# The skip term of y moved from a TensorE matmul to ScalarE, the convolution carries gathered on GpSimd, and a whole third B product on GpSimd in nine groups

## The chip, the cores and the metric

The kernel runs on one core of a Trainium2 chip. The core has TensorE (PE, matrix products into PSUM), VectorE (DVE), ScalarE (ACT), GpSimd (POOL) and SyncE (SP, which issues DMAs); each works through its own instruction stream in order and waits for the others on semaphores. The metric is the device time of one execution, in microseconds; lower is better.

## The reference

Two blocks follow each other on x of shape (2, 1024, 512). The first is a Mamba block; only its middle matters here:

```python
xs, res = jnp.split(xn @ W_in, 2, axis=-1)            # 1024 channels each
xs = silu(causal_conv(xs, conv_w) + conv_b)            # 4 taps, depthwise
delta = softplus(dt_r @ W_dt + b_dt)
h = h * exp(delta * A) + delta * B * u                 # scan over time, 16 states a channel; u = xs
y = einsum(h, C) + u * D                               # the skip term is u * D
y = y * silu(res);  out = y @ W_out + x
```

The second block is a mixture of 32 experts (top 4 of 32, 2048 tokens, and a shared expert). The change does not touch it.

## The kernel before, in words

Time is cut into NSEG = 4 segments of 512 steps (two for each sequence), and the 1024 channels into DC = 8 tiles of 128 partitions. One pair of segment s and tile d is a group, g = 8s + d, from 0 to 31. The scans go through the groups one after the other, each with its 16 states in four quarters q of 4 states. For one group the engines do this:

- ScalarE: `decay(g, q)` writes four factors exp(delta * A) into four PSUM banks `da`, each as soon as VectorE has done with the bank's last content; `silu_z` and `silu_x` need another activation table, so a table load stands ahead of and behind them; `tap` makes the first of the four convolution taps of a tile of the next segment; `softplus` makes the next group's delta; `spread_du` copies `du` into PSUM.
- VectorE: `spread(g, q)` makes du * B for a quarter (128x2048), `scans(g, q)` runs four scans (L945), `gate(g-1)` multiplies the last group's y by silu(res), and `conv` makes the other three taps (L914, each waits for the one before it).
- GpSimd: `weigh(g, q)` multiplies a quarter by C (L1342, and folds it in two in some groups, L1347), `delta_x` makes delta and du for the next group, and `spread` makes the quarters that `by_pool` gives to it.
- TensorE: `summed(g, q)` adds the quarter's four states into the bank `y_ps` with an identity matrix (L1542), and between the quarters it runs the work of `gap_items`: input projections for the next segment ("in", L1439), its gate projection ("z", L1471), delta ("dt", L1476), output projections of the last segment ("out", L1461), transposes. A float32 product of 128x512 stands in the trace as two matmul records, so a block of four is a row of x8.

Who makes a product with B depends on the group. `dense` groups (d = 3, 4, 5 of segments 0 to 2: groups 3, 4, 5, 11, 12, 13, 19, 20, 21) carry most of the "in" items and so the convolutions. `leaving` groups (d = 0 to 2 of segments 1 to 3) carry the "out" items. Ahead of its quarter 0 each group has the skip term: TensorE waits for `gate(g-1)`, which frees `y_ps`, and multiplies the diagonal matrix `d_diag` by xs (L1539).

A segment with s even is the first half of a sequence; there VectorE also makes the carry into the next segment, three small instructions for each tile that stand between the taps (L908). In odd segments it adds this carry to the first three columns (L911).

The order of each engine's work is written out in the program's loops over g and q; no planner moves it. The functions that the change touches, and what calls them:

## Time and profile before

| | |
|---|---|
| median of 3 runs | 1617.28 us (1613.62 to 1618.94) |
| profiled execution, its own time | 1620.9 us |
| its span in the profile | 1618.9 us |
| busy in the span | PE 1449.8, DVE 1308.3, ACT 741.5, POOL 1077.6 us |
| the scans of groups 0 to 31 | from 72 to 996 us of the span |

Busy time is a mean over stages with different limits. The scans take the first 996 us; the rest is the routing and the experts. Times in rows are microseconds from the start of the span; a row such as "4.57 ... [0.16 <-ACT bank L717]" says that the instructions took 4.57 us and that the engine had stood idle for 0.16 us before, until ScalarE's line 717 released it.

### The profile page before, as it was taken

Reading aid. Unit: us, or ns where it says so; the run is one execution under the profiler, and the core shown is the slowest. Engines: PE = TensorE matmul, PEld = TensorE weight load, DVE = VectorE, ACT = ScalarE, POOL = GpSimd, SP = SyncE. Lnnn points to the kernel's source line nnn. Section 1 sums busy time; section 2 is a strip of 40 time slices with the busy share of each in tenths; the row PEclk is TensorE's granted clock in tenths of the full one; section 3 lists DMA queues with packets and bytes.
Section 4 is the critical chain, followed back from the end, with each engine's and each line's share of the span. In section 5 each row is a group of like instructions: output and inputs, shape, how many; then the busy total and the mean of one; then the engine's idle time right before and its main releaser. Section 6 shows DMA issues by size and latency. Waiting matters only on the chain. (4 is left out here: it accounts for less than half of the span.)

```text
span 1618.9 us, 14732 instructions
## 1 busy us (share of the span) xinstructions
PE 1449.8 (90%) x4412; PEld 725.0 (45%) x4413; DVE 1308.3 (81%) x1931; ACT 741.5 (46%) x1160; POOL 1077.6 (67%) x545
## 2 busy tenths in 40 slices
PE   6578998889998889998798878899998999999996
PEld 3233443334443334443343323444445766667774
DVE  4599999999999999999999997355636777777772
ACT  4566665776656776657566664421000111111111
POOL 0199898999887999989999997230011455555453
PEclk9889999899999999999899999999999999999998
DMA  4540112410113411103310004021412888888895
GB/s 131 221 174 9 42 48 101 179 40 30 35 47 108 171 41 36 35 15 126 129 36 21 28 1 156 20 104 33 182 54 64 225 237 225 218 239 223 259 260 68
DMA packets 63823, 176.86 MB, mean 109 GB/s; under 512 B 10304, under 2 KB 15168, under 8 KB 55040
## 3 DMA queue, kind: packets, MB, share of 16 engines
q1 hardware_dynamic: 48128, 138.59, 24.8%
q0 software_dynamic: 15616, 37.32, 11.1%
q8 instruction: 37, 0.61, 0.2%
q14 instruction: 42, 0.34, 0.1%
HBM read 142.98 MB, written 32.85 MB: 109 GB/s over the span
## 5 line engine op out<-in xcount | busy, mean ns | idle before, releaser
L1342 POOL TENSOR_TENSOR h<-h,c_rep 128x2048 f32<-128x2048 f32 x128 | 579.3, 4530 | 31.2 <-DVE h L945 26.1
L1542 PE MATMUL bank<-h,ident 128*128 128x512 f32 x916 | 449.3, 634 | 93.0 <-POOL h L1342 74.2
L717 ACT ACTIVATE bank<-delta,a_neg 128x512 f32<-128x512 f32 x512 | 335.8, 682 | 178.9 <-DVE h L945 178.1
L1542 PEld LDWEIGHTS bank<-h,ident 128*128 128x128 f32 x916 | 180.6, 202 | 335.9 <-issue 210.9
L945 DVE TENSOR_TENSOR_SCAN h<-bank,state,h 128x512 f32<-128x512 f32 x256 | 306.0, 1260 | 0.5 <-ACT bank L717 0.5
L945 DVE TENSOR_TENSOR_SCAN h<-bank,h 128x512 f32<-128x512 f32 x256 | 290.7, 1199 | 2.8 <-ACT bank L717 2.6
L171 DVE STREAM_TRANSPOSE xT<-xg 32x256 f32<-32x256 f32 (+1 forms) x592 | 247.3, 418 | 56.0 <-DMA xg<-flat,slot_token 48.3
L935 DVE TENSOR_TENSOR h<-bank,b_rep 128x2048 f32<-128x2048 f32 (+1 forms) x105 | 227.5, 2184 | 35.7 <-ACT bank L708 24.2
L1703 POOL DMA_INDIRECT out<-y,slot_token x64 | 101.8, 1590 | 110.1 <-DMA out<-y,slot_token 65.2
L1329 POOL TENSOR_TENSOR h<-du,b_rep 128x2048 f32<-128x2048 f32 (+1 forms) x32 | 125.4, 3920 | 11.5 <-PE bank L1542 11.5
L1787 ACT ACTIVATE y<-y_ps,share 128x512 f32<-128x512 f32 x69 | 47.4, 687 | 185.3 <-PE y_ps L1935 152.3
L1439 PE MATMUL bank<-xnT,w_in 128*128 128x512 f32 x256 | 120.4, 616 | 10.1 <-ACT zs L680 9.2
L1893 PE MATMUL g_ps<-xT,w_ring 128*128 128x256 f32 x512 | 119.4, 387 | 8.2 <-issue 4.3
L1471 PE MATMUL bank<-xnT,w_res 128*128 128x512 f32 x256 | 118.6, 607 | 0.1
L1461 PE MATMUL bank<-w_out,xs 128*128 128x512 f32 x256 | 115.6, 594 | 1.5 <-DVE xs L955 0.9
L1893 PEld LDWEIGHTS g_ps<-xT,w_ring 128*128 128x128 f32 x512 | 98.9, 194 | 38.1 <-issue 25.6
L1893 PE MATMUL u_ps<-xT,w_ring 128*128 128x256 f32 x512 | 115.7, 379 | 0.0
L1935 PE MATMUL y_ps<-w_ring,act 128*128 128x512 f32 x256 | 115.4, 594 | 0.0
L1893 PEld LDWEIGHTS u_ps<-xT,w_ring 128*128 128x128 f32 x512 | 96.9, 190 | 13.0
L1695 POOL DMA_INDIRECT xg<-flat,slot_token x65 | 64.9, 998 | 50.9 <-POOLq L411 25.6
L1407 POOL DMA_INDIRECT xg<-flat,slot_token x4 | 4.0, 1012 | 135.4 <-DVE slot_token L1210 134.5
L1439 PEld LDWEIGHTS bank<-xnT,w_in 128*128 128x128 f32 x256 | 49.9, 197 | 76.6 <-issue 62.4
(238 smaller groups left out, 1530.0 us busy)
## 6 DMA issues: line engine op xcount, KB each, us to landing
w_ring<-in_w SPq DMA_DIRECT2D x32, 1024.0 KB, 5.3
b_rep<-bcd SPq DMA_DIRECT2D x16, 1024.0 KB, 6.9
c_rep<-bcd SPq DMA_DIRECT2D x16, 1024.0 KB, 5.0
w_ring<-in_w SPq DMA_DIRECT2D x32, 512.0 KB, 7.4
w_in<-in_w_in_x SPq DMA_DIRECT2D x32, 256.0 KB, 2.6
w_res<-in_w_in_res SPq DMA_DIRECT2D x32, 256.0 KB, 2.6
xa<-in_x SPq DMA_DIRECT2D x20, 256.0 KB, 3.0
xb<-in_x SPq DMA_DIRECT2D x16, 256.0 KB, 3.0
```

Source lines behind the costliest of these rows:

```text
L171: ins = eng.transpose(out[cols:cols + PIECE, 0:slots, :, rows:rows + PIECE], x[rows:rows + PIECE, :, :, cols:cols + PIECE])
L717: eng.activation(da[j][:], delta[:, g % 2], ACT.Exp, scale=a_neg[:, col:col + 1])\
L935: eng.tensor_tensor(h[:, q, a:b], du_ps[:].unsqueeze(1).to_broadcast([P, b - a, SEG]), b_rep[:, Q * q + a:Q * q + b, :], ALU.mult).then_in ...
L945: eng.tensor_tensor_scan(h[:, q, j, :], da[j][:], h[:, q, j, :], init, ALU.mult, ALU.add)\
L1329: eng.tensor_tensor(h[:, q, a:b], du[:].unsqueeze(1).to_broadcast([P, b - a, SEG]), b_rep[:, Q * q + a:Q * q + b, :], ALU.mult).then_inc(S ...
L1342: ins = eng.tensor_tensor(h[:, q], h[:, q], c_rep[:, Q * q:Q * q + Q, :], ALU.mult)
L1439: ins = eng.matmul(out[:], w_in[:, n % 2, k, :], xnT[:, s % 2, k, :], start=(k == 0), stop=(k == KC - 1))
L1461: eng.matmul(out[:], xs[:, s % 2, d, i * P:(i + 1) * P], w_out[:, d, :], start=(d == 0), stop=False)
L1471: ins = eng.matmul(out[:], w_res[:, i % 2, k, :], xnT[:, s % 2, k, :], start=(k == 0), stop=(k == KC - 1))
L1542: ins = eng.matmul(y_ps[:], c.ident[:], h[:, q, j, :], start=False, stop=(q == NQ - 1 and j == Q - 1))
L1893: ins = eng.matmul(out[:, f * 2 * P:(f + 1) * 2 * P], c.w1r[:, own, k, first + f * P:first + (f + 1) * P], xT[:, u % 2, k, :], start=(k == ...
L1935: ins = eng.matmul(y_ps[i][:], turned[:, k, v * P:(v + 1) * P], c.w2r[:, places(n)[0] % RING, k, :], start=(k == 0), stop=(k == FC - 1))
```

## The change

The change has three parts.

1. The skip term. In place of the matmul with `d_diag`, ScalarE writes xs times D straight into `y_ps` (`skip_term`), once `gate(g-1)` is done, and TensorE's sums then add to what stands there. ScalarE does it in each group but the first, behind `decay(g, 2)` and ahead of the taps and of `softplus`. Only one of the eight diagonal blocks is still made.
2. The carries. In even segments ScalarE copies the last three columns of each convolution input to `conv_edge` right behind the tap, and GpSimd makes the carries of all eight tiles at once in six small instructions (`tails`), in groups 1 and 17. VectorE's three small instructions for each tile go.
3. The third quarter's B product in the nine dense groups: GpSimd makes all four states, where before it made two and VectorE the other two.

```diff
@@ -128,6 +128,7 @@
         b_dt, d_skip = new("b_dt_sb", [P, DC]), new("d_skip", [P, DC])
         a_neg, norm_w = new("a_neg", [P, DC * NS]), new("norm_w_a", [P, KC])
         tail, bc, state = new("conv_tail", [P, DC, KW - 1]), new("bc", [P, P]), new("state", [P, DC * NS])
+        edge, part = new("conv_edge", [P, DC, KW - 1]), new("conv_part", [P, KW - 1, DC, KW - 1])
         st6, mv = new("st6", [P, NSEG, ST, 6]), new("mv", [P, NSEG, ST, 2])
         eps_ln, eps_rms, minus = new("eps_ln", [P, 1]), new("eps_rms", [P, 1]), new("minus", [P, ST])
         lnv, rvar, ms = new("lnv", [P, ST]), new("rvar", [P, ST]), new("ms", [P, ST])
@@ -228,11 +229,11 @@
         gu_ps = [(bank[0], bank[1]), (bank[2], bank[3])]
         PLACED, RESTED, LISTED = E, 2 * E, 2 * E + 2 * REST
 
-        names = ("const_ready small_loaded aneg_ready diag_ready xp_loaded out_loaded stat_done mv_ready ln_chain "
+        names = ("const_ready small_loaded aneg_ready diag_ready xp_loaded out_loaded stat_done carry_made mv_ready ln_chain "
                  "rvar_ready ms_ready rrms_ready scales_ready pool_chain xn_ready tap_done "
                  "conv_chain xs_ready bcd_written sp_chain sp_ready delta_ready "
                  "du_made du_ready bq_made b3_made da_ready scan_done state_saved weighed cmul_done y_summed gate_done "
-                 "xr_ready").split()
+                 "xr_ready skip_made").split()
         S = {n: sem("m_" + n) for n in names}
         b_loaded = [sem(f"m_b_loaded{q}") for q in range(NQ)]
         c_loaded = [sem(f"m_c_loaded{q}") for q in range(NQ)]
@@ -274,7 +275,7 @@
                 return (0, 0)
             if q == NQ - 1:
                 return (0, Q)
-            return (Q // 2, Q) if q == NQ - 2 and dense(g) else (0, 0)
+            return (0, Q) if q == NQ - 2 and dense(g) else (0, 0)
 
         def by_vector(g, q):
             a, b = by_pool(g, q)
@@ -666,8 +667,11 @@
 
                 def tap(s, j):
                     ps, _ = filled(eng, "in", s, j)
-                    eng.activation(xs[:, s % 2, j, :], ps[:], ACT.Identity, scale=conv_w[:, j, KW - 1:KW],
-                                   bias=conv_b[:, j:j + 1]).then_inc(S["tap_done"], 1)
+                    ins = eng.activation(xs[:, s % 2, j, :], ps[:], ACT.Identity, scale=conv_w[:, j, KW - 1:KW], bias=conv_b[:, j:j + 1])
+                    if s % 2 == 0:
+                        after(eng, S["carry_made"], s // 2 * 2 * (KW - 1))
+                        ins = eng.activation(edge[:, j, :], ps[:, SEG - KW + 1:SEG], ACT.Copy)
+                    ins.then_inc(S["tap_done"], 1)
 
                 def silu_x(s, j):
                     read(eng, "in", s, j)
@@ -698,6 +702,11 @@
                     eng.activation(spl[:], spl[:], ACT.Exp, scale=-1.0).then_inc(S["sp_chain"], 1)
                     eng.wait_ge(S["sp_chain"], g * 2 + 2)
                     eng.activation(spl[:], spl[:], ACT.Ln, bias=c.ones[:, 0:1]).then_inc(S["sp_ready"], 1)
+
+                def skip_term(g):
+                    s, d = divmod(g, DC)
+                    eng.wait_ge(S["gate_done"], g)
+                    eng.activation(y_ps[:], xs[:, s % 2, d, :], ACT.Copy, scale=d_skip[:, d:d + 1]).then_inc(S["skip_made"], 1)
 
                 def spread_du(g):
                     eng.wait_ge(S["du_made"], g + 1)
@@ -728,8 +737,7 @@
                 layer_var(1)
                 root_mean(1)
                 eng.wait_ge(c.made, 4)
-                for d in range(DC):
-                    ins = eng.activation(d_diag[:, d, :], c.ident[:], ACT.Copy, scale=d_skip[:, d:d + 1])
+                ins = eng.activation(d_diag[:, 0, :], c.ident[:], ACT.Copy, scale=d_skip[:, 0:1])
                 ins.then_inc(S["diag_ready"], 1)
                 for j in range(DC):
                     tap(0, j)
@@ -772,6 +780,8 @@
                     if d == DC - 1 and s + 2 < NSEG:
                         root_mean(s + 2)
                     decay(g, 2)
+                    if g:
+                        skip_term(g)
                     for it in gap_of(g - 1, 3, "in"):
                         tap(it[1], it[2])
                     for it in gap_of(g - 1, 3, "out", 1):
@@ -902,12 +912,8 @@
                     p, x, w = work[u], xs[:, s % 2, j, :], conv_w
                     eng.wait_ge(S["tap_done"], n + 1)
                     for sft in range(1, KW):
-                        if s % 2 == 0:
-                            k = KW - sft
-                            old = conv_b[:, j:j + 1].to_broadcast([P, KW - 1]) if sft == 1 else tail[:, j, 0:k]
-                            link(eng.scalar_tensor_tensor(tail[:, j, 0:k], p[:, SEG - k:SEG], w[:, j, sft - 1:sft], old,
-                                                          ALU.mult, ALU.add))
-                        elif sft == 1:
+                        if s % 2 and sft == 1:
+                            eng.wait_ge(S["carry_made"], (s // 2 + 1) * 2 * (KW - 1))
                             link(eng.scalar_tensor_tensor(x[:, 0:KW - 1], p[:, 0:KW - 1], w[:, j, KW - 1:KW], tail[:, j, :],
                                                           ALU.mult, ALU.add))
                             eng.wait_ge(S["conv_chain"], links[0])
@@ -1347,6 +1353,23 @@
                         ins = eng.tensor_tensor(h[:, q, 0:Q // 2], h[:, q, 0:Q // 2], h[:, q, Q // 2:], ALU.add)
                     ins.then_inc(S["cmul_done"], 1)
 
+                def tails(s):
+
+                    eng.wait_ge(S["tap_done"], (s + 1) * DC)
+                    made = s // 2 * 2 * (KW - 1)
+                    for sft in range(1, KW):
+                        k = KW - sft
+                        eng.tensor_tensor(part[:, sft - 1, :, 0:k], edge[:, :, sft - 1:KW - 1],
+                                          conv_w[:, :, sft - 1:sft].to_broadcast([P, DC, k]), ALU.mult).then_inc(S["carry_made"], 1)
+                    eng.wait_ge(S["carry_made"], made + KW - 1)
+                    eng.tensor_tensor(tail[:], part[:, 0], conv_b[:].unsqueeze(2).to_broadcast([P, DC, KW - 1]), ALU.add)\
+                        .then_inc(S["carry_made"], 1)
+                    for sft in range(2, KW):
+                        k = KW - sft
+                        eng.wait_ge(S["carry_made"], made + KW - 1 + sft - 1)
+                        eng.tensor_tensor(tail[:, :, 0:k], tail[:, :, 0:k], part[:, sft - 1, :, 0:k], ALU.add)\
+                            .then_inc(S["carry_made"], 1)
+
                 weighed = [0]
                 for s in (0, 1):
                     mean_square(s)
@@ -1356,6 +1379,8 @@
                     s, d = divmod(g, DC)
                     if d == DC - 1:
                         mean_square(s + 2)
+                    if d == 1 and s % 2 == 0:
+                        tails(s)
                     spread(g, 2)
                     weigh(g, 0)
                     spread(g, 3)
@@ -1532,14 +1557,16 @@
                     s, d = divmod(g, DC)
                     if g == 0 and q == 0:
                         was_free(eng, 5)
-                    if q == 0:
-                        after(eng, S["gate_done"], g)
+                    if q == 0 and g == 0:
                         eng.wait_ge(S["diag_ready"], 1)
                         eng.wait_ge(S["xs_ready"], g + 1)
                         eng.matmul(y_ps[:], d_diag[:, d, :], xs[:, s % 2, d, :], start=True, stop=False)
+                    elif q == 0:
+                        eng.wait_ge(S["skip_made"], g)
                     eng.wait_ge(S["cmul_done"], g * NQ + q + 1)
                     for j in range(Q // 2 if folded(g, q) else Q):
-                        ins = eng.matmul(y_ps[:], c.ident[:], h[:, q, j, :], start=False, stop=(q == NQ - 1 and j == Q - 1))
+                        ins = eng.matmul(y_ps[:], c.ident[:], h[:, q, j, :], start=False, stop=(q == NQ - 1 and j == Q - 1),
+                                         skip_group_check=g > 0)
                     ins.then_inc(S["y_summed"], 1)
 
                 for it in opening:
```

On ScalarE, in group 4, before (from `silu_z` to the last quarter's decays; `bank` is a PSUM bank, `zs` silu(res), `spl` and `delta` the parts of softplus):

```order
L680 ACTIVATE zs<-bank 128x512
L675 ACTIVATE xs<-xs 128x512 x3
L771 ACT_TABLE_LOAD
L717 ACTIVATE bank<-delta,a_neg 128x512 x4
L669 ACTIVATE xs<-bank,conv_b_sb,conv_w_sb 128x512
L695 ACTIVATE spl<-bank,b_dt_sb 128x512
```

and in the changed kernel, at the same place:

```order
L684 ACTIVATE zs<-bank 128x512
L679 ACTIVATE xs<-xs 128x512 x3
L779 ACT_TABLE_LOAD
L726 ACTIVATE bank<-delta,a_neg 128x512 x4
L709 ACTIVATE bank<-xs,d_skip 128x512
L670 ACTIVATE xs<-bank,conv_b_sb,conv_w_sb 128x512
L699 ACTIVATE spl<-bank,b_dt_sb 128x512
```

The skip term (L709) stands behind the four decays of quarter 2 and ahead of the tap.

On TensorE, in group 4, before (from the "dt" item of the group before to quarter 1's sums; `ident` is the identity matrix):

```order
L1476 MATMUL bank<-dtr,w_dt_sb 128x512
L1439 MATMUL bank<-xnT,w_in 128x512 x4
L1539 MATMUL bank<-xs,d_diag 128x512
L1542 MATMUL bank<-h,ident 128x512 x4
L1439 MATMUL bank<-xnT,w_in 128x512 x4
L1542 MATMUL bank<-h,ident 128x512 x4
```

and in the changed kernel:

```order
L1501 MATMUL bank<-dtr,w_dt_sb 128x512
L1464 MATMUL bank<-xnT,w_in 128x512 x4
L1568 MATMUL bank<-h,ident 128x512 x4
L1464 MATMUL bank<-xnT,w_in 128x512 x4
L1568 MATMUL bank<-h,ident 128x512 x4
```

The skip matmul is gone, and nothing else moved; the first sums now wait for ScalarE's L709.

On GpSimd, from quarter 3 of group 2 to quarter 0 of group 3 and on to quarter 3's product with B, before (`du` times `b_rep` is the product with B, `h` times `c_rep` the weighing with C):

```order
L1342 TENSOR_TENSOR h<-h,c_rep 128x2048
L1329 TENSOR_TENSOR h<-du,b_rep 128x1024
L1339 TENSOR_TENSOR state<-h,ones 128x4
L1342 TENSOR_TENSOR h<-h,c_rep 128x2048
L1329 TENSOR_TENSOR h<-du,b_rep 128x2048
```

and in the changed kernel:

```order
L1348 TENSOR_TENSOR h<-h,c_rep 128x2048
L1335 TENSOR_TENSOR h<-du,b_rep 128x2048
L1345 TENSOR_TENSOR state<-h,ones 128x4
L1348 TENSOR_TENSOR h<-h,c_rep 128x2048
L1335 TENSOR_TENSOR h<-du,b_rep 128x2048
```

The product with B ahead of quarter 0's weighing has twice the columns.

## Rows read from the trace of the kernel before

**Rows 1.** The page's strip of VectorE's busy tenths, 40 slices of the span

```profile
DVE  4599999999999999999999997355636777777772
```

**Rows 2.** Busy time by window, a window for each group: 3, 4, 11, 12, 13, 18, 19, 20

```profile
core 0: us, PE busy (x) PEld busy (x) DVE busy (x) ACT busy (x) POOL busy (x), PEclk, DMA share, GB/s
...
153.54:188.28 34.74, 34.74 (x82) 15.37 (x82) 31.52 (x33) 18.65 (x27) 34.26 (x14) 1.00 0.11 33
188.28:219.92 31.64, 29.72 (x69) 12.47 (x68) 31.16 (x33) 20.12 (x30) 27.08 (x13) 1.00 0.12 36
...
391.31:424.69 33.38, 33.38 (x78) 14.88 (x79) 32.61 (x39) 19.98 (x31) 33.21 (x10) 1.00 0.14 42
424.69:457.83 33.14, 31.15 (x69) 13.43 (x68) 32.62 (x40) 20.09 (x30) 27.84 (x9) 0.95 0.12 34
457.83:487.96 30.13, 28.14 (x62) 12.08 (x61) 29.99 (x33) 19.31 (x29) 25.26 (x8) 0.94 0.15 46
...
600.40:630.02 29.62, 28.15 (x64) 12.40 (x64) 27.43 (x22) 18.75 (x30) 28.90 (x14) 0.94 0.06 20
630.02:664.49 34.47, 33.23 (x76) 14.38 (x77) 31.46 (x34) 20.04 (x32) 33.91 (x16) 1.00 0.15 40
664.49:696.13 31.64, 30.29 (x70) 12.78 (x69) 31.17 (x33) 20.11 (x30) 28.33 (x13) 1.00 0.12 36
```

**Rows 3.** Timeline of VectorE in group 4: start, us, engine, line

```profile
192.76 1.20 DVE L935 TENSOR_TENSOR h<-bank,b_rep 128x1024 f32<-128x1024 f32 x1
...
199.16 4.57 DVE L945 TENSOR_TENSOR_SCAN h<-bank,h 128x512 f32<-128x512 f32 x4 [0.16 <-ACT bank L717]
...
215.49 2.32 DVE L914 SCALAR_TENSOR_TENSOR xs<-bank,conv_w_sb,xs 128x511 f32<-128x511 f32 x3
```

**Rows 4.** Timeline of ScalarE in group 4

```profile
198.34 2.52 ACT L717 ACTIVATE bank<-delta,a_neg 128x512 f32<-128x512 f32 x4
...
214.20 0.78 ACT L669 ACTIVATE xs<-bank,conv_b_sb,conv_w_sb 128x512 f32<-128x512 f32 x1 [1.49 <-PE bank L1439]
```

**Rows 5.** Timeline of TensorE in group 4

```profile
195.53 3.70 PE L1439 MATMUL bank<-xnT,w_in 128*128 128x512 f32 x8 [1.62 <-ACT zs L680]
199.06 1.12 PE L1539 MATMUL bank<-xs,d_diag 128*128 128x512 f32 x2
...
210.57 3.60 PE L1439 MATMUL bank<-xnT,w_in 128*128 128x512 f32 x8
```

**Rows 6.** ScalarE's groups by line and shape: busy us, mean ns, idle before

```profile
L708 ACT ACTIVATE bank<-du 128x512 f32<-128x512 f32 x32 | 19.2, 600 | 75.4 <-POOL du L1318 75.4
...
L1787 ACT ACTIVATE y<-y_ps,share 128x512 f32<-128x512 f32 x67 | 46.0, 687 | 183.2 <-PE y_ps L1935 150.2 <-PE y_ps L1879 23.4 <-DMA out<-y,slot_token 8.1
```

**Rows 7.** Timeline of TensorE at 432 and at 751 us, a block behind an idle stretch

```profile
432.18 5.40 PE L1439 MATMUL bank<-xnT,w_in 128*128 128x512 f32 x8 [1.99 <-ACT zs L680]
...
751.48 3.70 PE L1542 MATMUL bank<-h,ident 128*128 128x512 f32 x8 [2.73 <-POOL h L1342]
```

**Rows 8.** Timeline of VectorE in group 11, one convolution with its carries

```profile
407.15 0.19 DVE L908 SCALAR_TENSOR_TENSOR conv_tail<-bank,conv_w_sb,conv_b_sb 128x3 f32<-128x3 f32 x1
...
409.74 4.80 DVE L945 TENSOR_TENSOR_SCAN h<-bank,state,h 128x512 f32<-128x512 f32 x4
```

**Rows 9.** GpSimd's products with B by shape, scans of all groups

```profile
L1329 POOL TENSOR_TENSOR h<-du,b_rep 128x2048 f32<-128x2048 f32 x23 | 104.1, 4528 | 10.5 <-PE bank L1542 10.5
...
L1329 POOL TENSOR_TENSOR h<-du,b_rep 128x1024 f32<-128x1024 f32 x9 | 21.3, 2366 | 1.0 <-PE bank L1542 1.0
```

**Rows 10.** Timeline of GpSimd in group 3, then early in group 17

```profile
175.71 1.27 POOL L1318 TENSOR_TENSOR du<-delta,xs 128x512 f32<-128x512 f32 x1 [0.17 <-POOL delta L1314]
...
577.34 0.21 POOL L1339 TENSOR_TENSOR state<-h,ones 128x4 f32<-128x4 f32 x1
577.63 4.52 POOL L1342 TENSOR_TENSOR h<-h,c_rep 128x2048 f32<-128x2048 f32 x1
```

**Rows 11.** Timeline of VectorE: opening, and end of group 3

```profile
51.74 0.22 DVE L908 SCALAR_TENSOR_TENSOR conv_tail<-bank,conv_w_sb,conv_b_sb 128x3 f32<-128x3 f32 x1 [2.15 <-ACT xs L669]
...
179.22 2.28 DVE L935 TENSOR_TENSOR h<-bank,b_rep 128x2048 f32<-128x2048 f32 x1
```

## The prediction

> **What bounds the kernel now.** I read the strip of busy tenths first: VectorE is at nine tenths or more through nearly all of the scans [rows 1]. That says who is busy, not who sets the pace, so I cut the scans into one window for each group [rows 2]. The reader is to see three kinds there. In groups 3 and 11 TensorE is busy the whole window (34.74 of 34.74 us, 33.38 of 33.38) and GpSimd nearly so (34.26, 33.21), while VectorE is not. In groups 4, 12, 13 and 20 VectorE has all but 0.1 to 0.5 us, GpSimd has 3.3 to 5.3 us to spare and TensorE only 1.4 to 2.0. In group 18 GpSimd is the fullest (28.90 of 29.62). So each part of the change meets a group in which its receiver has no room, and what VectorE is relieved of counts only where nobody else comes last. For that I read the timeline of group 4.
>
> **The half product with B that VectorE loses.** It is one instruction of 1.20 us at 192.76, in each of nine groups [rows 3]. The next scans but four start at 199.16 and already wait 0.16 us for ScalarE's decays [rows 3], whose batch starts at 198.34 [rows 4]. That batch stands behind two table loads and three silus that start once quarter 0's scans are through, ahead of the half product. Without the half product VectorE only waits longer, 1.3 instead of 0.16 us. The gain in groups 4, 5, 20 and 21 is nothing; in groups 12 and 13, whose scans are longer, I take 0.15 us each. The bound below is that all 9 x 1.1 = 9.9 us are lost as gain, the bound above that they are kept.
>
> **The skip term.** TensorE saves the two records at 199.06, about 1.0 us, in 31 groups. But it started its sums behind them at 200.05, and now waits for ScalarE, where the skip term stands behind the whole batch of decays: 198.34 + 2.52 = 200.86 [rows 4, 5]. No activation from SBUF to PSUM with a scale of its own stands in the trace for Copy; between 0.60 us (a plain copy from SBUF into PSUM) and 0.69 us (a copy with a scale out of PSUM) [rows 6] I take 0.65. So the sums start at about 201.6, 1.5 us later. (The Trainium skill, "ScalarE: Activation LUTs", section "Rules for kernel authors", budgets about 0.3 us for each activation and 0.83 ns an element, which makes an estimate of 0.72 us for 512; by it each such group would be 0.07 us longer still. The rows here are shorter, so I keep them.)
>
> Who waits for these sums? Four blocks of TensorE follow without a gap (sums, "in", sums, "in"), the last at 210.57 for 3.60 us; ScalarE's tap waited 1.49 us for it at 214.20, and VectorE's convolution at 215.49 came right behind [rows 3 to 5]. The tap ends at 214.98 and the taps of the convolution start 0.5 us later with a small instruction (0.2 us) between, so only 0.3 us is slack, and closer packing of the blocks gives 0.2 more. Groups 4 and 20 become 1.5 - 0.5 = 1.0 us longer each. In group 12 the same chain is met by carries that leave VectorE: a convolution with its carries takes 409.74 - 407.15 = 2.59 us, three taps alone 2.32 less the overlap, 2.23, so 0.36 us for each convolution [rows 3, 8]; the copy of the edge adds about 0.2 us to the tap. I take -0.2 us for group 12, and for group 13, whose two convolutions have slack behind TensorE, -0.15 - 0.7 = -0.8. In groups without convolutions the gate comes behind the decays, and skip copy (0.65) and skip matmul (1.0) change places with nothing behind them late: 0.
>
> **The clock.** The wait opens an idle stretch on TensorE that was not there. Its "in" block starts when ScalarE frees the bank (195.53 [rows 5]) and ends near 199.1; then it idles until 201.6, 2.5 us. What such a stretch does the trace shows both ways: behind 1.99 us of idleness eight records took 5.40 us, in a group whose mean granted clock is 0.95, not 1.00 [rows 2, 7], so part of them ran at 1.2 in place of 2.4 GHz; behind 2.73 us they took 3.70 [rows 7]. At 5.40 the chain above is 1.75 us longer. I take the fall for the three groups 4, 12 and 20, 5.25 us, and 0.5 us in each of 5, 13 and 21, where the block is followed by a convolution that has over a microsecond of slack, 1.5 us. The bounds are 0 and 6.75.
>
> **The whole product on GpSimd.** Twice the states cost 4.53 - 2.37 = 2.16 us in each of nine groups [rows 9]. Groups 4, 12, 13 and 20 leave GpSimd 3.3 to 5.3 us idle [rows 2], most of it right behind this product, where it waits for quarter 0's scans, and groups 5 and 21 are built alike: 0. In the first group of each run GpSimd comes from a full stretch and hands the 2.16 us on through weigh 0, spread 3 and weigh 1 to du. In group 3 du ended at 176.98, its copy would end at 177.6 and VectorE took it at 179.22 [rows 10, 11]: 1.6 us slack, 0.6 late; TensorE's second sums, which wait for weigh 1, then delay "in" and the third convolution a little more: +0.8. In group 11 TensorE has no idle time at all [rows 2], so its second sums come 1.8 us late and "in", tap and third convolution with them; the carries give back 0.3: +1.5. Group 19 follows groups that GpSimd already fills: +2.0. Sum 4.3, bounds 0 and 3 x 2.16 = 6.5, and 3.4 more if TensorE's clock falls in groups 11 and 19, where it would idle some 2.1 us ahead of its second sums.
>
> **The carries on GpSimd.** Six instructions of 0.20 us, of which some wait for the one before: such a pair has a pitch of 0.29 us (577.34 to 577.63 [rows 10]); between 6 x 0.20 and 6 x 0.29 I take 1.4. In group 17 they stand exactly in this gap, on the fullest engine, and what VectorE and TensorE do through group 18 follows it: +1.4. In group 1 GpSimd waits for TensorE behind them: +0.2. In the opening VectorE waited 2.15 us ahead of each convolution [rows 11], so the carries that it no longer makes count only in the last tile: -0.2.
>
> **Sum.** Without the clock 2.0 - 0.2 - 0.8 + 4.3 + 1.4 + 0.2 - 0.2 = 6.7 us, with it 6.7 + 6.75 = 13.4 us. Against the profiled execution's own 1620.9 that is 1634.3. This execution lies 3.6 us above the median of the runs shown, 1617.28, so a median of 1631 is what I forecast.
>
> **The rivals.**
> (a) The clock does not fall in the new gaps: +6.7, 1624. For it speaks the row at 751 us, against it the one at 432 [rows 7]. It shares its chance, 0.24, over +2 to +10 us.
> (b) The other side: VectorE is the bound and keeps what it is relieved of. Then 9 x 1.1 for the half products and 24 x 0.12 for the carries in the scans come off, 12.8 us: 1604.5. What decides is the start of TensorE's first sums in group 4: if they start no later than 11.8 us behind the group's first scan, as now, and the third batch of scans before 10.9 us, this is right. For it speaks the strip [rows 1] and VectorE's 31.16 of 31.64; against it the 0.16 us [rows 3]. Chance 0.12.
> (c) Each engine's slack eats both sides, within 4.8 us: 1617. The saved 1.0 us of TensorE in the groups with "out" items, where it is nearly full too (28.15 of 29.62 in group 18 [rows 2]), would pay for the delays. Chance 0.12.
> (d) The clock falls in groups 11 and 19 too, and GpSimd's delay passes in full: 13.4 + 3.4 + 2.2 = +19, 1636. Chance 0.10.
> The forecast itself, +10 to +17: 0.42.
>
> **How the numbers follow.** A measurement of this kernel tells 0.3%, 4.9 us, from no change. Faster: (b), 0.12. Same: (c) and a third of (a), 0.20. Slower: 0.68. The range for 8 in 10 leaves out most of (b) and the far end of (d): 1613 to 1637. The forecast's own is 1627 to 1634.
>
> **What would show it.** Right: the first sums of group 4 start about 13.3 us behind its first scan, VectorE waits over 1 us for ScalarE ahead of the third batch of scans in groups 4, 5, 20 and 21, and again for the tap ahead of the third convolution; groups 4 and 20 last 34 us, or 32.7 if the clock holds; group 19 about 36.5; group 17 and 18 together 1.4 us more. Wrong: groups 4 and 20 at 30.5 us, or a skip activation that starts before the decays' batch has ended.

## The result: 0.9% slower, as forecast

The changed kernel takes 1631.36 us (median of 6 runs, 1627.62 to 1632.17), the kernel before 1616.53 us in 6 runs beside it (1613.62 to 1618.94). The ratio is 1.0088, 95% interval 1.0067 to 1.011. The forecast was 1631 with 1613 to 1637. (Two single runs lie far outside all others, 1928.11 us of the kernel before and 5172.87 us of the kernel with the three mends below; the ratios leave them out, the medians hold them.)

The profiled execution took 1631.55 us, its span is 1629.9. I read the windows first, one for each group, the same groups as [rows 2], with 28 behind them:

```profile
core 0: us, PE busy (x) PEld busy (x) DVE busy (x) ACT busy (x) POOL busy (x), PEclk, DMA share, GB/s
155.44:191.11 35.67, 33.84 (x79) 14.49 (x79) 30.39 (x33) 19.27 (x28) 35.19 (x14) 1.00 0.11 32
191.11:225.60 34.49, 31.14 (x69) 13.30 (x68) 30.24 (x33) 20.63 (x31) 31.66 (x13) 0.95 0.11 33
396.11:431.23 35.12, 34.20 (x75) 14.69 (x76) 30.54 (x30) 19.47 (x31) 34.95 (x11) 0.95 0.13 38
431.23:465.62 34.39, 30.71 (x68) 13.10 (x67) 30.55 (x30) 20.80 (x34) 30.33 (x9) 0.95 0.11 33
465.62:494.97 29.35, 25.36 (x59) 10.86 (x58) 28.19 (x27) 19.96 (x32) 27.07 (x8) 1.00 0.16 48
607.95:639.20 31.25, 28.04 (x62) 12.38 (x62) 27.55 (x23) 19.35 (x32) 30.05 (x14) 0.89 0.06 19
639.20:675.63 36.43, 32.63 (x74) 13.92 (x75) 30.38 (x33) 19.91 (x30) 35.87 (x16) 1.00 0.13 38
675.63:710.11 34.48, 31.12 (x69) 13.28 (x68) 30.23 (x33) 20.63 (x31) 31.67 (x13) 0.95 0.11 33
905.24:933.85 28.61, 21.96 (x43) 8.92 (x42) 26.21 (x21) 16.96 (x25) 24.98 (x8) 0.88 0.04 12
```

In group 4 VectorE was busy for all but 0.48 us; now it is idle for 4.25 of 34.49 us. It does 0.9 us less and the group lasts 2.85 us longer. In groups 3 and 19 GpSimd fills the window (35.19 of 35.67, 35.87 of 36.43), and TensorE, which was full in group 3, is not any more: the bound has changed engines.

The timelines of group 4 answer to [rows 3 to 5]. VectorE:

```profile
191.06 9.01 DVE L951 TENSOR_TENSOR_SCAN h<-bank,h 128x512 f32<-128x512 f32 x8
199.99 0.66 DVE L961 TENSOR_TENSOR xs<-bank,zs 128x512 f32<-128x512 f32 x1
201.92 4.57 DVE L951 TENSOR_TENSOR_SCAN h<-bank,h 128x512 f32<-128x512 f32 x4 [1.26 <-ACT bank L726]
...
220.87 0.22 DVE L917 SCALAR_TENSOR_TENSOR xs<-bank,conv_w_sb,conv_tail 128x3 f32<-128x3 f32 x1 [2.10 <-ACT xs L670]
```

ScalarE:

```profile
201.13 2.53 ACT L726 ACTIVATE bank<-delta,a_neg 128x512 f32<-128x512 f32 x4
203.59 0.67 ACT L709 ACTIVATE bank<-xs,d_skip 128x512 f32<-128x512 f32 x1
...
220.05 0.78 ACT L670 ACTIVATE xs<-bank,conv_b_sb,conv_w_sb 128x512 f32<-128x512 f32 x1 [3.15 <-PE bank L1464]
```

TensorE:

```profile
198.31 3.70 PE L1464 MATMUL bank<-xnT,w_in 128*128 128x512 f32 x8 [1.04 <-ACT zs L684]
204.32 5.40 PE L1568 MATMUL bank<-h,ident 128*128 128x512 f32 x8 [2.31 <-ACT bank L709]
...
216.42 3.60 PE L1464 MATMUL bank<-xnT,w_in 128*128 128x512 f32 x8
```

Read them across. The gate (L961) has freed `y_ps` at 200.65. The skip term starts at 203.59, because it stands behind four decays, which stand behind the table load. TensorE waits for it, 2.31 us, and then runs its eight records in 5.40 us. The "in" block at 216.42 comes 25.36 us behind the first scan (before: 210.57 against 188.28, 22.29), the tap waits 3.15 us for it, and the convolution waits 2.10 us for the tap. The 1.20 us product that VectorE no longer makes comes back as the 1.26 us that it waits for the third batch of decays.

The other end of the change, GpSimd in group 17 and VectorE in group 19:

```profile
584.34 0.59 POOL L1362 TENSOR_TENSOR conv_part<-conv_edge,conv_w_sb 128x24 f32<-128x24 f32 x3
585.01 0.23 POOL L1365 TENSOR_TENSOR conv_tail<-conv_part,conv_b_sb 128x24 f32<-128x24 f32 x1
585.31 0.52 POOL L1370 TENSOR_TENSOR conv_tail<-conv_tail,conv_part 128x16 f32<-128x16 f32 x2
585.78 0.20 POOL L1345 TENSOR_TENSOR state<-h,ones 128x4 f32<-128x4 f32 x1
```

```profile
658.18 4.57 DVE L951 TENSOR_TENSOR_SCAN h<-bank,h 128x512 f32<-128x512 f32 x4 [1.91 <-POOL h L1335]
...
666.23 2.29 DVE L941 TENSOR_TENSOR h<-bank,b_rep 128x2048 f32<-128x2048 f32 x1 [1.02 <-ACT bank L717]
```

The carries take 585.78 - 584.34 = 1.44 us with nothing else beside them. In group 19 VectorE waits 1.91 us for GpSimd's product, in a place where it waited for nobody before (there its scans followed a convolution without a wait, at 647.81).

The sum over the groups, from the group lengths of both traces: 3, 4, 5 +4.4 us; 11, 12, 13 +2.2; 17 and 18 +1.6; 19 +2.0; 20, 21 +3.5. That makes +13.7. All other groups together -2.1, the stretch ahead of the scans +1.7, behind them -2.4: the span is 11.0 us longer.

### The profile page after: what moved, and what is told of

It reads as the page before. It is cut to its first block and busy times, and to the rows that moved or that the text cites. A ratio compares the mean times of both kernels' runs of the same rounds, so it can differ in the third digit from the quotient of the medians.

```text
span 1629.9 us, 14619 instructions
## 1 busy us (share of the span) xinstructions
PE 1433.8 (88%) x4350; PEld 717.0 (44%) x4351; DVE 1293.4 (79%) x1874; ACT 758.5 (47%) x1200; POOL 1099.5 (67%) x557
## 5 line engine op out<-in xcount | busy, mean ns | idle before, releaser
L1568 PE MATMUL bank<-h,ident 128*128 128x512 f32 x916 | 462.7, 650 | 144.6 <-POOL h L1348 81.6
L941 DVE TENSOR_TENSOR h<-bank,b_rep 128x2048 f32<-128x2048 f32 x96 | 216.6, 2278 | 35.6 <-ACT bank L717 14.0
L1335 POOL TENSOR_TENSOR h<-du,b_rep 128x2048 f32<-128x2048 f32 x32 | 144.8, 4525 | 13.1 <-PE bank L1568 12.9
L920 DVE SCALAR_TENSOR_TENSOR xs<-bank,conv_w_sb,xs 128x511 f32<-128x511 f32 (+2 forms) x96 | 71.8, 747 | 25.6 <-ACT conv_edge L673 22.8
```

The costliest lines, as they stand in the source:

```text
L941: eng.tensor_tensor(h[:, q, a:b], du_ps[:].unsqueeze(1).to_broadcast([P, b - a, SEG]), b_rep[:, Q * q + a:Q * q + b, :], ALU.mult).then_in ...
L1335: eng.tensor_tensor(h[:, q, a:b], du[:].unsqueeze(1).to_broadcast([P, b - a, SEG]), b_rep[:, Q * q + a:Q * q + b, :], ALU.mult).then_inc(S ...
L1568: ins = eng.matmul(y_ps[:], c.ident[:], h[:, q, j, :], start=False, stop=(q == NQ - 1 and j == Q - 1), skip_group_check=g > 0)
```

## The experiments

Each was compared with runs of the kernel before on the same chip; ratios are to those: 28 runs, median 1619.51, for the three parts and the early skip term; 19 runs, 1617.27, for the filler, the half product in three groups, the earlier carries and the three mends; 29 runs, 1618.32, for the last three. The changed kernel itself had 1616.53 beside it, so medians of different sets are not subtracted from each other here. One kernel's runs lie up to 19 us apart and the intervals are 3 to 6 us wide on each side, so I judge each edit by the lengths of the groups it touches and use the ratio for the whole.

### One part at a time

**The skip term alone**, on the kernel before:

```diff
                     decay(g, 2)
+                    if g:
+                        skip_term(g)
...
-                    if q == 0:
-                        after(eng, S["gate_done"], g)
+                    if q == 0 and g == 0:
...
+                    elif q == 0:
+                        eng.wait_ge(S["skip_made"], g)
```

> The kernel before with the skip term alone moved to ScalarE. Theory (the skip term stands behind the decays, TensorE's sums come late and its clock falls in the new gap): about +8 us against before, with groups 4 and 20 at 34 to 34.5 us in place of 31.6 and group 12 near 34.5. Rival A (the loss of the change comes from GpSimd's added work alone): within 2 us of before. Rival B (TensorE is relieved and that pays): 5 us or more faster than before.

Measured: 1623.79 us, 1.0029 (0.9997 to 1.0061). Windows of groups 3, 4 and 20, then TensorE in group 4:

```profile
153.99:187.88 33.89, 33.89 (x79) 14.79 (x79) 31.43 (x34) 19.26 (x28) 33.41 (x14) 1.00 0.12 34
187.88:220.67 32.79, 29.05 (x68) 12.50 (x67) 31.27 (x34) 20.73 (x31) 29.08 (x13) 1.00 0.11 35
...
665.08:699.56 34.48, 30.86 (x68) 13.08 (x67) 31.37 (x34) 20.61 (x31) 29.24 (x13) 0.95 0.13 33
```

```profile
201.12 3.70 PE L1549 MATMUL bank<-h,ident 128*128 128x512 f32 x8 [2.30 <-ACT bank L705]
```

The wait is there, and costs 32.79 - 31.64 = 1.15 us without the clock. The fall behind it is not certain: the 2.30 us are followed by 3.70 us here, and group 20, of the same build, has a window at 0.95 that is 1.7 us longer. Group 3 shows what my sum lacked: TensorE is busy 33.89 of 33.89 us there, so the missing matmul shortens the group by 0.9 us.

**The whole B product alone:**

```diff
-            return (Q // 2, Q) if q == NQ - 2 and dense(g) else (0, 0)
+            return (0, Q) if q == NQ - 2 and dense(g) else (0, 0)
```

> The kernel before with the whole third B product on GpSimd in the nine dense groups, nothing else. Theory: groups 3, 11 and 19 get 1 to 2 us longer each, groups 4, 5, 20, 21 stay at 31.6 and 29.2 because ScalarE's decays come last, groups 12 and 13 gain 0.15 each: +3 to +4 us. Rival (VectorE keeps what it is relieved of): -8 to -10 us.

Measured: 1621.08 us, 1.0015 (0.9999 to 1.003). Groups 3 and 4:

```profile
153.56:189.20 35.64, 34.72 (x80) 14.90 (x80) 30.50 (x32) 18.64 (x27) 35.16 (x14) 1.00 0.12 32
189.20:220.82 31.62, 30.18 (x70) 12.86 (x69) 30.04 (x33) 20.12 (x30) 30.44 (x13) 1.00 0.13 36
```

Rival (b) falls here: with nothing else changed VectorE is relieved of 1.1 us in group 4 (30.04 against 31.16 busy) and the group lasts 31.62 us against 31.64. Groups 5, 20 and 21 are unchanged too. Group 12 gains 0.4, and that is a wait of VectorE for the tap, seen below, which the kernel before had and this build has not. Group 3 is 0.9 us longer, group 11 2.1, groups 17 to 19 together 1.6.

**The carries alone** (part 2 of the change):

```diff
+                    if s % 2 == 0:
+                        after(eng, S["carry_made"], s // 2 * 2 * (KW - 1))
+                        ins = eng.activation(edge[:, j, :], ps[:, SEG - KW + 1:SEG], ACT.Copy)
...
+                    if d == 1 and s % 2 == 0:
+                        tails(s)
```

> The kernel before with the carries alone moved to GpSimd. Theory: groups 12 and 13 lose 0.7 us each and group 11 0.3, group 17 with 18 gains 1.4 us: about 0 (-1 to +1) in all. Rival (what leaves VectorE is gained, and GpSimd's six small instructions are free): -3 us.

Measured: 1619.51 us, 1.0 (0.9981 to 1.002). Groups 12, 17 and 18:

```profile
424.56:456.16 31.60, 29.85 (x70) 12.81 (x69) 31.39 (x30) 20.30 (x33) 27.63 (x9) 1.00 0.12 36
...
568.43:599.61 31.18, 28.67 (x62) 12.57 (x62) 27.54 (x22) 19.56 (x31) 30.23 (x20) 0.89 0.16 53
599.61:627.54 27.93, 26.45 (x64) 11.82 (x64) 27.45 (x22) 19.13 (x31) 27.21 (x14) 1.00 0.07 21
```

Groups 17 to 19 are 2.6 us longer together, of which 1.44 are the six instructions; a clock of 0.89 in group 17 and 0.95 in 19 stand beside the rest. Group 12 is 1.5 us shorter. Here are one of its three convolutions and the start of the third on VectorE in the kernel before:

```profile
447.85 0.19 DVE L908 SCALAR_TENSOR_TENSOR conv_tail<-bank,conv_w_sb,conv_b_sb 128x3 f32<-128x3 f32 x1
...
450.43 2.28 DVE L935 TENSOR_TENSOR h<-bank,b_rep 128x2048 f32<-128x2048 f32 x1
453.02 0.22 DVE L908 SCALAR_TENSOR_TENSOR conv_tail<-bank,conv_w_sb,conv_b_sb 128x3 f32<-128x3 f32 x1 [0.31 <-ACT xs L669]
```

and the same convolution with the carries alone moved:

```profile
447.33 2.29 DVE L914 SCALAR_TENSOR_TENSOR xs<-bank,conv_w_sb,xs 128x511 f32<-128x511 f32 x3
449.55 2.28 DVE L935 TENSOR_TENSOR h<-bank,b_rep 128x2048 f32<-128x2048 f32 x1
```

The convolution takes 2.58 us from start to start in the one and 2.22 in the other, and VectorE, which waits for nobody in this group now, keeps that three times: 1.1 us. The other 0.4 us are the wait for the tap: the block of 5.40 us that the kernel before had at 432.18 [rows 7] took 3.70 here, and the tap no longer comes late. With the product alone no block of group 12 ran slow either, and it is 0.4 us shorter (32.72). Group 13, with two convolutions, is 0.75 us shorter.

The three parts alone add up to 0.4% in the ratios and the whole measures 0.9%. In the groups of the forecast they make 5.8, 4.0 and 0.3 us, 10.1 of 13.7. The missing 3.6 us are a balance. Group 4 is 1.7 us longer than its parts make it, because its block behind the new wait ran slow here and not with the skip term alone. Group 12 is 3.2 us longer: 1.6 are such a slow block, and the other 1.6 come because the late sums hold the group at 32.8 us (as the filler below shows), where the carries alone had brought it to 31.60. Group 3 adds 0.9, because GpSimd's delay covers what the missing matmul gave. Groups 11 and 17 to 19 take 2.3 back.

### Mending one part of the changed kernel

**The skip term earlier.** In groups 4 and 5 of each of the first three segments ScalarE writes it behind the first of the four decays, when the gate has just ended:

```diff
+                def early(g):
+                    return g // DC < NSEG - 1 and g % DC in (4, 5)
                 def decay(g, q):
                     for j in range(Q):
+                        if q == 2 and j == 1 and early(g):
+                            skip_term(g)
...
-                    if g:
+                    if g and not early(g):
                         skip_term(g)
```

> The changed kernel, but in groups 4, 5, 12, 13, 20 and 21 the skip term stands behind the first of the four decays of quarter 2 in place of behind the fourth. Theory: TensorE's first sums start about 11.5 us behind the group's first scan in place of 13.2, the idle stretch ahead of them shrinks from 2.3 to 0.6 us, the clock stays up, and groups 4, 12 and 20 come back to 31.5 to 32 us: 8 us faster than the changed kernel, still some 5 us slower than before. Rival (the place of the skip term does not matter, GpSimd sets the pace): within 2 us of the changed kernel.

Measured: 1623.85 us, 1.0027 (0.9997 to 1.0058). Groups 4 and 12, and TensorE in group 4:

```profile
189.42:221.07 31.65, 29.82 (x68) 12.32 (x67) 30.08 (x32) 20.73 (x31) 30.47 (x13) 1.00 0.12 36
...
427.01:458.58 31.57, 29.68 (x69) 12.60 (x68) 30.34 (x29) 20.91 (x34) 30.11 (x9) 1.00 0.12 36
```

```profile
200.83 3.70 PE L1573 MATMUL bank<-h,ident 128*128 128x512 f32 x8 [0.47 <-ACT bank L709]
```

The moved line gives back 2.8 us in each of groups 4, 12 and 20, 34.49 to 31.65 in group 4, and 0.65 in each of 5 and 21, with everything else left in: 9.8 us. That is the cause of the largest term, shown by taking it away. For the whole the ratio falls from 1.0088 to 1.0027, which is 9.9 us, with intervals of 3 to 5 us on each side. This profiled execution was one of the kernel's longest (1630.63 us of 1613.68 to 1632.45): it has groups 7, 16, 19 and 30 1.3 to 1.7 us longer than the changed kernel's, which the edit doesn't touch.

**The clock alone.** The wait stays, but TensorE is given less idleness: two redundant matmuls ahead of the "in" block, overwritten by the block itself:

```diff
+                        if s > 0 and i in (3, 6):
+                            for _ in range(2):
+                                eng.matmul(out[:], w_in[:, n % 2, 0, :], xnT[:, s % 2, 0, :], start=True, stop=True)
```

> The changed kernel with two more matmuls (four records, 1.7 us, their result overwritten) ahead of the input projection that TensorE does just before the idle stretch of groups 4, 5, 12, 13, 20 and 21. The sums can start no earlier by it; TensorE is only busy for longer before. Theory (the fallen clock is 1.75 us of each of groups 4, 12 and 20): the stretch shrinks from 2.3 to 0.6 us, the first sums take 3.6 and not 5.3 us, 5 us faster than the changed kernel. Rival (the late start alone costs, the clock is hidden): no faster, up to 2 us slower.

Measured: 1627.95 us, 1.0061 (1.0037 to 1.0085). Group 4, and TensorE in it:

```profile
188.78:221.57 32.79, 31.15 (x73) 13.45 (x72) 30.14 (x33) 20.73 (x31) 31.63 (x13) 1.00 0.11 35
```

```profile
196.02 1.98 PE L1465 MATMUL bank<-xnT,w_in 128*128 128x512 f32 x4 [1.05 <-ACT zs L684]
197.84 3.60 PE L1467 MATMUL bank<-xnT,w_in 128*128 128x512 f32 x8
202.03 3.70 PE L1571 MATMUL bank<-h,ident 128*128 128x512 f32 x8 [0.59 <-ACT bank L709]
```

The sums start 13.2 us behind the first scan, as in the changed kernel, but take 3.70 us. Group 4 is 1.70 us shorter and groups 12 and 20 are 1.6 and 1.7. So of the 2.85 us in group 4, 1.15 are the delay and 1.70 the clock. One group alone could not show that the filler did it, for group 4 lasts 32.79 us without a filler too, with the skip term alone and with the carries earlier. All six places do: behind 2.3 us of idleness 12 of 18 such blocks ran slow (5 of 6 in the changed kernel, 3 with the half product, 4 with the carries earlier), behind 0.59 us none of 6. The ratio of the whole does not stand apart from that of the changed kernel; the verdict rests on the groups.

**The half product again in groups 3, 11 and 19:**

```diff
-            return (0, Q) if q == NQ - 2 and dense(g) else (0, 0)
+            return (Q // 2 if g % DC == 3 else 0, Q) if q == NQ - 2 and dense(g) else (0, 0)
```

> The changed kernel, but in groups 3, 11 and 19 GpSimd makes only half of the third B product again. Theory: groups 3 and 11 lose 1 to 1.5 us each, group 19 2 us: 4 us faster than the changed kernel. Rival (the whole product costs in all nine groups alike, or nowhere): 1.4 us or less.

Measured: 1629.36 us, 1.0048 (1.001 to 1.0087). Groups 3 and 19:

```profile
153.12:187.00 33.88, 33.88 (x79) 14.78 (x79) 31.42 (x34) 19.25 (x28) 33.40 (x14) 1.00 0.12 34
634.23:668.47 34.24, 32.38 (x74) 14.00 (x75) 31.26 (x33) 19.91 (x30) 33.68 (x16) 1.00 0.15 41
```

Group 3 is 1.8 us shorter, group 19 2.2, group 11 1.0. (Groups 12 and 21 are shorter too, 1.6 and 0.7, where the edit does nothing: their blocks behind the wait took 3.70 here.) In group 3 it is not the 34.7 us of the kernel before that comes back but 33.88, TensorE full again and one matmul short. The two parts had hidden each other: the skip term's 0.9 us and GpSimd's 1.8.

**The carries of the second sequence three groups earlier**, in group 14 in place of 17. GpSimd is idle there for 4.4 of 28.77 us in the changed kernel:

```diff
-                    if d == 1 and s % 2 == 0:
-                        tails(s)
+                    if g == 1:
+                        tails(0)
+                    if g == 2 * DC - 2:
+                        tails(2)
```

> The changed kernel, but the six small carry instructions of segment 2 stand in group 14, where GpSimd has some 4 us idle, in place of group 17. Theory: 1.4 us of groups 17 to 19 go, group 14 keeps its length: 1.4 us faster than the changed kernel. Rival (they were hidden in group 17 too): no difference.

Measured: 1628.5 us, 1.006 (1.0042 to 1.0079). Group 14 lasts 28.78 us against 28.77, and groups 17 to 19 together are 2.1 us shorter (95.07 against 97.17), more than the 1.44 us moved; group 17 runs at a clock of 1.00 here against 0.94. TensorE in groups 4 and 20 of this one execution:

```profile
203.27 3.70 PE L1570 MATMUL bank<-h,ident 128*128 128x512 f32 x8 [2.31 <-ACT bank L709]
...
682.64 5.40 PE L1570 MATMUL bank<-h,ident 128*128 128x512 f32 x8 [2.30 <-ACT bank L709]
```

The same block behind the same wait, once at the high and once partly at the low clock. The edit does not touch either place.

### All mends together, and beyond

**The three mends in one kernel** (skip term early, half product in 3, 11 and 19, carries in 14), and the same kernel once more:

> The changed kernel with three mends: the skip term behind the first decay in the six groups with three or more silus, half the third product on GpSimd in groups 3, 11 and 19, the carries of segment 2 in group 14. Theory: 8 + 4 + 1.4 us faster than the changed kernel, that is 0 to 2 us faster than before, since half a microsecond to one of the removed matmul is kept in groups 3, 11 and 19. Rival (the mends overlap): 5 us slower than before or more.

> The kernel with the three mends once more, on the chip of the two beside it, for a narrower interval: 2 to 5 us faster than before; if its gain was chance, within 1 us of before.

Measured: 1614.79 us, 0.9967 (0.9941 to 0.9992), and 1616.23 us, 0.9985 (0.9967 to 1.0003). Group 7 and group 30 of the first execution, then of the second:

```profile
273.52:300.72 27.20, 19.66 (x44) 8.20 (x43) 25.13 (x21) 20.21 (x34) 25.34 (x18) 0.94 0.64 244
...
943.00:971.59 28.59, 21.94 (x43) 8.89 (x42) 26.21 (x21) 16.95 (x25) 24.96 (x8) 0.88 0.00 0
```

```profile
275.85:305.68 29.83, 23.84 (x48) 10.01 (x47) 25.22 (x21) 19.93 (x34) 26.60 (x18) 0.84 0.60 227
...
946.42:973.33 26.91, 18.84 (x43) 7.95 (x42) 26.10 (x22) 17.13 (x25) 24.98 (x8) 0.97 0.00 0
```

With the three costs taken away the 0.9% is gone: no interval reaches above 1.0003, with the rest of the change left in. In groups 17 to 19, though, the mends do not add up. Alone the half product takes 2.2 of 97.17 us off and the earlier carries 2.1, together only 1.9 and 2.7 in the two executions, with a clock of 0.91 in group 19; this stays open.

One and the same kernel, and group 7 differs by 2.6 us, group 30 by 1.7 the other way, each time with the lower clock at the longer one. The whole change is worth 15 us, and where the falls land moves 2 to 3 us in a single group that nobody edited.

**The half product in all nine groups**, with the other two mends: is there any gain in the six groups where GpSimd has room?

```diff
-            return (Q // 2 if g % DC == 3 else 0, Q) if q == NQ - 2 and dense(g) else (0, 0)
+            return (Q // 2, Q) if q == NQ - 2 and dense(g) else (0, 0)
```

> The kernel with the three mends (skip term behind the first decay in six groups, half the third product in groups 3, 11 and 19, carries of segment 2 in group 14), but GpSimd makes half of the third product in all nine groups, as before the change; VectorE makes the other half. Theory (in groups 4, 5, 20 and 21 ScalarE's decays come last, so the half product on VectorE is free): groups 4, 5, 20, 21 within 0.1 us of 31.65 and 29.16, groups 12 and 13 up to 0.2 us longer, in all within 1 us of the kernel with the three mends. Rival (the whole product in six groups is what gains): 5 to 6 us slower than it.

Measured: 1620.84 us, 1.0012 (0.9991 to 1.0032). Groups 4, 5, 20 and 21 are 0.1 us longer than with the whole product, 12 and 13 0.3 each: 1.0 us for 6 x 1.1 us of VectorE's work. The medians are 4.6 us apart, more than that, but the intervals overlap. The profiled executions do not show where it lies. The one with the half products is 2.7 us the shorter of the two (1617.18 against 1619.93): its scans take 4.6 us longer, with groups 1, 28 and 30, which the edit does not touch, at 29.16, 28.60 and 29.88 us against 27.61, 26.91 and 26.90, and what follows the scans takes 6.0 us less. What separates the medians stays open.

**Redundant matmuls where the clock fell**: two ahead of quarter 2's sums, in the next "z" item's bank, in the last group of each segment and from 27 on:

```diff
+                def refill(g):
+                    it = ("z", (g + 1) // DC, g + 1, 0)
+                    out = work[begin(it)]
...
+                    for _ in range(2):
+                        eng.matmul(out[:], w_res[:, it[2] % 2, 0, :], xnT[:, it[1] % 2, 0, :], start=True, stop=True)
...
+                        if q == 2 and g < LAST and (g % DC == DC - 1 or g // DC == NSEG - 1 and g % DC > 2):
+                            refill(g)
```

> The kernel with the three mends, and in groups 7, 15, 23 and 27 to 30 TensorE makes two more matmuls (four records, 1.7 us, overwritten by the gate projection that follows) ahead of quarter 2's sums, where it stands idle for 2.3 to 3.5 us waiting for GpSimd. Theory (how long the other groups take differs from kernel to kernel by 1.7 us at a time because the clock falls in some of these idle stretches and not in others, and GpSimd's third product waits for the sums behind them): no group of 27 to 30 over 27 us, at least one of them was 28.6; groups 7 and 23 no longer than 28.5; 2 to 5 us faster than the kernel with the three mends. Rival (the 1.7 us steps have another cause): the steps stay, and the two matmuls change nothing or cost up to 1 us a group.

Measured: 1610.25 us, 0.9952 (0.9934 to 0.9969), the fastest version here, faster than the kernel before and so than the changed one too. Groups 7, 28 and 30:

```profile
273.74:300.93 27.19, 21.35 (x48) 8.90 (x47) 25.13 (x21) 20.21 (x34) 25.32 (x18) 0.94 0.64 244
...
887.85:914.76 26.91, 22.25 (x47) 9.06 (x46) 26.10 (x22) 17.13 (x25) 24.98 (x8) 0.94 0.05 12
941.66:968.58 26.92, 20.55 (x47) 8.49 (x46) 26.11 (x22) 17.13 (x25) 25.00 (x8) 1.00 0.00 0
```

None of 28 to 30 has the 28.6 us that they had in the changed kernel or in one of the two executions before. Group 23 stayed at 29.91 us, where at most 28.5 was expected, and group 27 at 27.63, where 27 was, so it does not help everywhere. Over the same kernel without it on the same chip the gain is 6.0 us in the medians of 12 runs each. That the kernel is faster is measured; from which groups it comes is not shown, for in the second execution of the kernel without it groups 28 and 30 had no fall either.

## Why the prediction was right, step by step

**The bound.** That each group has its own, and that VectorE's busy share says nothing of it, held in all three kinds of group.

**The half product, 0 in groups 4, 5, 20, 21.** Right: VectorE waited 1.26 us where 1.3 was said, and the product alone changed those groups by at most 0.03 us. Groups 12 and 13 were taken at 0.15 each; against the half product in the mended kernel the whole one is worth 0.3. (With the product alone group 13 gained 0.02 and group 12 nothing that is not the tap's wait.)

**The skip term.** The activation took 0.673 us on the mean of 31, I had taken 0.65; the estimate of 0.72 us from the Trainium skill, "ScalarE: Activation LUTs", section "Rules for kernel authors", was further off, and the measurement decides. The sums of group 4 started 13.26 us behind its first scan, said was 13.3. The delay cost 1.15 us where 1.0 was said. What this step missed is the matmul that is gone: where TensorE has no idle time it is worth 0.9 us in group 3 and, where no block ran slow (32.69 us in the first execution of the mended kernel against 33.39 before), 0.7 in group 11. In group 3 GpSimd covers it in the changed kernel, so that term did not suffer; in group 11 it hid an error, as said below.

**The clock.** The fall in groups 4, 12 and 20 (1.70, 1.56 and 1.71 us), taken as 1.75 each, is in the profile and shown by its removal. It is a chance and not a price, though: the same blocks ran slow in 12 of 18 cases, and three out of three is partly luck. Group 13 had a fall of 0.5 us in the sum; its block stands behind the same 2.31 us of idleness and took 3.70, and the group is 0.78 us shorter, which is the -0.8 said without the fall. With the carries earlier that block did take 5.40 and the group lasted 29.87 us in place of 29.35, so the size was right. Groups 5 and 21 are 0.65 us longer each, said was 0.5. Group 12 came out at +1.26 where 1.55 was said, and by the reason given: without a slow block it lasts 32.83 us (filler), -0.3 against before where -0.2 was said, and the fall behind the wait is 1.56.

**The whole product in 3, 11, 19.** Said +0.8, +1.5, +2.0, measured +0.93, +1.74, +1.96. Group 11 fits partly by luck. The product alone cost 2.07 us there, more than the sum had; the missing matmul, which the sum did not have, gives 0.7 of it back; and at its start four records took 3.49 us (at 396.30; four of the filler took 1.98), in a window of 0.95.

**The carries.** 1.44 us for 1.4 said; groups 17 and 18 +1.57. The opening was said to gain 0.2 and the scans start 1.7 us later. I can't attribute this: over the executions of all kernels here the scans start between 69.5 and 73.9 us, and with the carries alone at 72.28, 0.1 us later than before.

**Groups without convolutions, 0.** This is the step that failed. They changed by -2.1 us in all, by up to 2 us in single groups of either sign (group 7 29.25 to 27.21, group 27 27.37 to 26.07, group 28 26.90 to 28.61), with the window's clock 1.00 for 0.85 in group 7 and 0.88 for 0.94 in group 28. Here is the block at the start of group 28 on TensorE:

```profile
904.72 5.40 PE L1568 MATMUL bank<-h,ident 128*128 128x512 f32 x8 [2.30 <-POOL h L1348]
```

TensorE waits for GpSimd before most sums there, and whether the block behind runs slow changes from kernel to kernel and, as the two executions of the mended kernel show, with no edit at all. Not each slow block costs: group 28 of the kernel before has one too, 5.40 us behind 2.34 us at 912.66, and lasts 26.90 us. In the groups that it named the sum was right to 0.3 us (13.7 for 13.4). The rest, -2.1, +1.7 and -2.4 us, was not in it. It made the profiled difference 10.7 us (1631.55 against 1620.9) where 13.4 was said, while the medians differ by 14.8: that the forecast median is met to 0.4 us is partly luck.

**Rivals.** (a) fell in the changed kernel, where five of six blocks ran slow, but 5 of 12 such blocks in two of its variants held the clock. (b) fell with the product alone. (c) is half true: slack eats nearly all that VectorE gains by the half products, but not what it gains by the carries (1.1 and 0.75 us in groups 12 and 13, alone), and none of the losses. (d): group 11 did run at 0.95 where it had 1.00, but its slow records stand at its start and not behind the wait for the second sums (3.70 us at 418.70); group 19 ran at 1.00.

## What to carry to other kernels

An operation that another engine waits for belongs at the point in its engine's stream where its input has just become ready, not behind the batch that happens to stand there: here three decays' difference was 2.8 us in each of three groups, 1.15 of it the delay and the rest the clock that fell in the wait. Work taken from the busiest engine is worth something only where that engine is not about to wait, and costs its full price where the receiver has no gap, so cut the time into windows and hand it over in those groups alone. Idle stretches of 2.3 us on TensorE cost up to 1.7 us more in the block behind them where the chain hangs on that block; a few redundant matmuls into a bank that is overwritten next bought that back in three groups here.

## What the runs showed of the hardware

Idle stretches of TensorE of 2.30 us were followed by eight records in 5.40 us or in 3.70, in the same place of kernels that differ elsewhere, and even within one execution; behind 0.47 to 0.80 us in those places all took 3.70. The same kernel profiled twice had it in different groups. The Trainium skill, "TensorE: Matmul & The Clock Gate", section "Part 1: The HAM clock gate (the "warmup" mystery)", says that one kernel shows different numbers of slow matmuls from run to run; the traces here agree, with group 7 at a granted clock of 0.94 and 0.84. A forecast of such a fall is therefore a chance for each place, and it moves single groups of one kernel by 2 to 3 us. It is not shown to be all of the scatter between runs (the mended kernel: 1609.50 to 1621.02 us). Behind the scans, in code that no edit touches, the profiled executions of all kernels here take 615.8 to 625.7 us; the four shortest of these stretches (up to 619.3) have a mean granted clock of 0.990 to 0.992, the nine others 0.982 to 0.986. Whether the clock is the cause there was not tested.
